# A graph network: the middle stage in pairs of tiles inside the last convolution round, and one table made in a later stage

## The reference

```python
h = jnp.maximum(_layernorm(x, axis=-1), 0.0)
x = x + _L0_gnn_ref(h, src, dst, ...)      # APPNP (5 hops), two GIN layers, mish
h = jnp.maximum(_layernorm(x, axis=-1), 0.0)
x = x + _L1_gnn_ref(h, edge_attr_3, ...)   # embedded edges, 2 x (edge MLP, sum by dst, node MLP)
h = jnp.maximum(_layernorm(x, axis=-1), 0.0)
x = x + _L2_gnn_ref(h, edge_index, ...)    # weighted sum over edges, by source
h = jnp.maximum(_layernorm(x, axis=-1), 0.0)
x = x + _L3_gnn_ref(h, src, dst, ...)      # typed features, sum by destination
```

```python
out = _gin(out, src, dst, eps2[0], W2, b2)   # ((1 + eps) * h + sum over neighbours) @ W2 + b2
return out * jnp.tanh(jax.nn.softplus(out))  # mish
```

## Time and profile before

| what | value |
|---|---|
| median of 3 runs | 4323.43 us |
| profiled execution, span | 4322.8 us |
| PE, DVE, POOL, ACT busy in the span | 73%, 59%, 49%, 31% |
| last convolution round | from 1585 us |
| middle stage | 1687.4 to 1789.2 us |
| first edge pass | 1789.2 to 2373 us |
| first node stage | 2373 to 2464 us |

### The profile page before, as it was taken

How to read it: one execution, slowest core, us unless ns; L and a number is a source line. 1 busy time by engine, 2 the same in 40 slices (tenths; PEclk the granted TensorE clock), 3 DMA queues, 4 the chain that set the end, 5 groups by cost and what they waited for, 6 DMA issues and landing times. The chain is left out here.

```text
span 4322.8 us, 75741 instructions
## 1 busy us (share of the span) xinstructions
PE 3164.4 (73%) x18619; PEld 2197.0 (51%) x18633; DVE 2559.5 (59%) x9496; ACT 1354.4 (31%) x2970; POOL 2139.2 (49%) x2173
## 2 busy tenths in 40 slices
PE   2488885669999996499998599998555555655554
PEld 1366662235666663377776367776333333333332
DVE  7688886985555554688887577776632222422223
ACT  0077886941111000255554355555300000200000
POOL 0477772000000002477774277776367777177776
PEclk7579998989999998699999799999655555755555
DMA  2112222000000002466666354455122212422223
GB/s 59 41 55 70 76 73 85 2 18 15 16 17 17 16 15 65 125 176 177 182 175 131 87 133 129 129 128 100 29 66 53 53 53 51 136 53 53 53 53 52
DMA packets 248700, 326.41 MB, mean 76 GB/s; under 512 B 78159, under 2 KB 159646, under 8 KB 247518
## 3 DMA queue, kind: packets, MB, share of 16 engines
q1 hardware_dynamic: 180122, 205.51, 15.7%
q0 software_dynamic: 68256, 117.02, 12.6%
HBM read 230.08 MB, written 92.25 MB: 75 GB/s over the span
## 5 line engine op out<-in xcount | busy, mean ns | idle before, releaser
L2506 PE MATMUL gat_acc<-gat_rows,gat_hot 128*128 128x128 f32 x1664 | 574.2, 478 | 489.1 <-issue 243.2
L2506 PEld LDWEIGHTS gat_acc<-gat_rows,gat_hot 128*128 128x128 f32 x1664 | 400.3, 317 | 664.3 <-issue 663.5
L971 PE MATMUL hop_p_a<-hop_h,adj 128*128 128x384 bf16 x4375 | 713.9, 327 | 0.0
L971 PEld LDWEIGHTS hop_p_a<-hop_h,adj 128*128 (+1 forms) x4375 | 428.7, 98 | 284.9 <-issue 2.5
L1914 POOL DMA_INDIRECT lb_far<-far_rows,lb_idx x416 | 407.2, 979 | 195.6 <-issue 118.6
L2489 POOL DMA_INDIRECT gat_rows<-typed_rows,gat_idx x416 | 396.0, 952 | 216.1 <-DVE gat_idx L2514 89.6
L2489 POOL DMA_INDIRECT gat_rows<-hidden_rows,gat_idx x416 | 395.8, 951 | 197.8 <-PE gat_acc L2506 78.0
L1914 POOL DMA_INDIRECT la_far<-far_rows,la_idx x416 | 410.5, 987 | 153.8 <-issue 117.7
L1630 POOL DMA_INDIRECT by_src_records<-scatter_rec,scatter_rank x375 | 381.6, 1018 | 129.2 <-issue 101.2
L2522 DVE TENSOR_SCALAR gat_hot<-iota_row,gat_tabs 128x128 f32<-128x128 f32 x416 | 148.6, 366 | 370.0 <-PE gat_acc L2506 363.9
L2519 DVE TENSOR_SCALAR gat_hot<-iota_row,gat_tabs 128x128 f32<-128x128 f32 x416 | 125.4, 307 | 392.7 <-PE gat_acc L2506 382.5
(11 more groups left out here) (501 smaller groups left out, 6395.6 us busy)
## 6 DMA issues: line engine op xcount, KB each, us to landing
edge_features<-emb_out SPq DMA_DIRECT2D x104, 256.0 KB
la_feat<-edge_features SPq DMA_DIRECT2D x104, 256.0 KB
edge_features<-la_out SPq DMA_DIRECT2D x104, 256.0 KB
lb_feat<-edge_features SPq DMA_DIRECT2D x104, 256.0 KB
la_place<-dst_row SPq DMA_DIRECT2D x104, 128.0 KB
lb_place<-dst_row SPq DMA_DIRECT2D x104, 128.0 KB
typed_rows<-gat_typed_row SPq DMA_DIRECT2D x25, 512.0 KB
cells_tabs<-x0share_nodes SPq DMA_DIRECT2D x125, 64.0 KB, 1.9
```

Of the source, the lines that this page charges most:

```text
L971: ins = nc.tensor.matmul(p_a[(u.par + r) % 2][:, 0:3 * D], K.adj[:, s, bass.ds(u.t * P, P)], h3[r % 2][:, s, :, :].rearrange("p i d -> p ( ...
L2506: nc.tensor.matmul(acc[:, bass.ds(at[u % LOADS], D)], hot[u % HOTS][:, :], rows[u % RING][:, :], start=False, stop=True, skip_group_check= ...
```

## The change

`gnn_input` is gone. Its work is done in `hops`, within the last round, in pairs of tiles (13 pairs, the last of one tile). The round is now written out for all 25 tiles on every engine. Buffers are cut out of the half of `h3` that the last round does not read, and so SP starts on x when the round before has been summed. Each pair's x and h are stored to DRAM (`dr.xn`, `dr.hn`) and loaded into `K.x` and `K.h` by SP in steps 1 to 21 of the first edge pass, together with the aggregate. The bias and the clip are DVE's now, and the inverse root is one power on POOL (2 columns) in place of the Newton steps. On PE the two products of a tile are one matmul of 256 columns. The tables by source are made in the first node stage: one PSUM bank is used by turns for the three transposed tables, whose transposes come in steps 3, 5 and 7 and whose copies come in steps 4, 6 and 8.

```diff
-            def gin2(u):
-                pe.wait_ge(s_a2, NT + u.t - 1)
-                products(u, HOPS + 1)
-            pipelined(pe, NT, gin2)
+            for t in range(NT + 5):
+                if t < NT:
+                    pe.wait_ge(s_a2, NT + t - 1)
+                    products(Turn(t, t % 2, t // 2, t < 2), HOPS + 1)
+                q = t // 2 - 2
+                if t % 2 == 0 and live(q):
+                    turned(q)
+                if t % 2 == 1 and live(q):
+                    weighed(q)
...
+            for t in range(2 * NP + 5):            # ACT
+                q = t // 2
+                if t % 2 == 0:
+                    norm(q - 2); high(q - 3); middle(q - 3)      # where live
+                else:
+                    exp(q); new_T(q - 2)
...
+            for q in range(NP):                    # POOL
+                c = width(q)
+                pool.wait_ge(s_num, q + 1)
+                nc.gpsimd.tensor_tensor(o[q % 2][:, 0:c, :], o[q % 2][:, 0:c, :], num[:, 0:c, :], ALU.mult).then_inc(s_on, 1)
+                pool.wait_ge(s_mish, q + 1)
+                pool.wait_ge(*x_sem(q))
+                nc.gpsimd.tensor_tensor(x_of(q), x_of(q), o[q % 2][:, 0:c, :], ALU.add).then_inc(s_x, 1)
+                pool.wait_ge(s_v, q + 1)
+                if q >= 2:
+                    pool.wait_ge(s_ln, q - 1)
+                nc.gpsimd.tensor_tensor(rstd[q % 2][:, 0:c], v[:, 0:c], K.neghalf[:, 0:c], ALU.pow).then_inc(s_root, 1)
...
+            for t in range(NT):                    # DVE
+                gin2(t)
+                q = t // 2
+                if t % 2 == 1:
+                    if live(q - 1):
+                        measured(q - 1)
+                    clipped(q)
+                    if live(q - 1):
+                        rooted(q - 1)
+                else:
+                    if live(q - 3):
+                        split_near(q - 3)
+                    if live(q - 1):
+                        mish(q - 1)
+                    if t == NT - 1:
+                        clipped(q)
+                    if live(q - 3):
+                        low(q - 3)
+            measured(NP - 2)
+            rooted(NP - 2)
+            mish(NP - 1)
+            measured(NP - 1)
+            rooted(NP - 1)
+            for q in range(NP - 3, NP):
+                split_near(q)
+                low(q)
...
+                if keeps and 1 <= g <= 3 * NB:     # SP, first edge pass
+                    t, q = (K.agg, K.h, K.x)[(g - 1) // NB], (g - 1) % NB
+                    lo, hi = QUADS[q][0], QUADS[q][-1] + 1
+                    sp.dma_start(t[:, lo:hi, :].rearrange("p t d -> p (t d)"),
+                                 (dr.agg, dr.hn, dr.xn)[(g - 1) // NB][:, lo * D:hi * D]).then_inc(s_node if g > NB else s_agg, 16)
...
+                    if keeps and g == 8:           # DVE, first edge pass
+                        dve.wait_ge(s_agg, NB * 16)
...
-                if last and r == 2:                # DVE, node stage
+                if r == 2:
                     table.vector(dve)
                 if last and r == 4:
                     table.outs(dve)
+                if not last and r in (4, 6, 8):
+                    table.outs(dve, (r - 4) // 2)
```

More of the change, by code:

```diff
@@ L506, with edge_tables @@
     pass
-def edge_tables(nc, K, dr, lay, ph, out=None, banks=None):
+def edge_tables(nc, K, dr, lay, ph, out=None, banks=None, shared=False):
     G, n_tab, S = lay.groups, lay.n_tab, lay.unit
@@ L529, in edge_tables @@
     if banks is None:
-        banks = [ph.ps(f"{lay.name}_tab_p_t{i}", [P, 4, P]) for i in range(n_tab * NB)]
+        banks = [ph.ps(f"{lay.name}_tab_p_t{i}", [P, 4, P]) for i in range(1 if shared else n_tab * NB)] * (n_tab if shared else 1)
     s_rec, s_ch, s_tab, s_tr, s_out, s_st, s_att = (ph.sem(f"{lay.name}_tab_{x}") for x in (
@@ L582, in vector, with outs @@
             nc.vector.tensor_copy(tab[:, 2, :], f(2)).then_inc(s_tab, 1)
-    def outs(dve):
-        for i in range(n_tab):
+    def outs(dve, only=None):
+        for i in range(n_tab) if only is None else (only,):
             dve.wait_ge(s_tr, i + 1)
@@ L591, in outs, with tensor @@
             ins.then_inc(s_out, 1)
-    def tensor(pe):
+    def tensor(pe, only=None):
         pe.wait_ge(s_tab, 1)
-        for i in range(n_tab):
+        for i in range(n_tab) if only is None else (only,):
+            if shared and i >= 1:
+                pe.wait_ge(s_out, i)
             for k in range(PT):
@@ L928, in hops @@
     s_a2, s_ch2 = (ph.sem(v) for v in ("gin_sum", "gin_chain"))
-    s_o = [ph.sem(f"o_stored{i}") for i in range(2)]
-    s_oc = ph.sem("o")
     dg = ph.ps("deg", [P, 32])
@@ L954, in _ @@
                 pipelined(sp, NT, load)
[L957 to L962, removed]
+                if r == 1:
+                    for j in range(2):
+                        sp.dma_start(w[:, j * D:(j + 1) * D], A["L1_gnn_eW1"][0, j * D:(j + 1) * D, :]).then_inc(s_w, 16)
+                    broadcast_row(sp, b2, A["L0_gnn_b2"], s_w)
@@ new lines, in measured @@
+            def measured(q):
+                c = width(q)
+                dve.wait_ge(s_x, q + 1)
+                for k in range(c):
+                    nc.vector.bn_stats(stats[:, k, :], x_of(q)[:, k, :]).then_inc(s_stats, 1)
+                dve.wait_ge(s_stats, PAIRS[q][-1] + 1)
+                if q >= 1:
+                    dve.wait_ge(s_rstd, q)
+                for k in range(c):
+                    nc.vector.bn_aggr(mv[:, k, :], stats[:, k, :]).then_inc(s_mv, 1)
+                dve.wait_ge(s_mv, PAIRS[q][-1] + 1)
+                nc.vector.tensor_scalar(v[:, 0:c], col(1, c), LN_EPS, None, ALU.add).then_inc(s_v, 1)
@@ L2016, in _ @@
             nc.vector.memset(K.sum[:, :, :], 0.0)
+            if keeps:
+                nc.vector.memset(K.x[:, NT:NW, :], 0.0)
             dve.wait_ge(s_w, W_LOADS * 16)
@@ L2143, in node_update @@
     PARTS = 1 if last else 2
-    table = edge_tables(nc, K, dr, dr.units, ph) if last else None
+    table = edge_tables(nc, K, dr, dr.units if last else dr.by_src, ph, shared=not last)
     LOADS = 9
@@ L2184, in _ @@
             cp = Chain(pool, s_pc)
-            if last:
-                table.gpsimd(pool)
+            table.gpsimd(pool)
             pool.wait_ge(s_ge, 16)
@@ L2279, in _ @@
                     product(r - TURN)
+                if not last and r in (3, 5, 7):
+                    table.tensor(pe, (r - 3) // 2)
         @block.scalar
```

423 lines of the change are left out of this document (191 added, 232 removed).

## The result

The changed kernel takes 4324.73 us, the median of nine runs (4322.38 to 4334.42), and the kernel before, in nine runs beside it, 4316.39 us (4312.15 to 4324.01). The ratio is 1.002, 95% interval 1.0011 to 1.003: slower by 8.3 us, where 58.8 us less were forecast. The profiled execution has the same span to a tenth as the one of before, because that one, 4323.4 us, lay 7 above the median of its nine.

What follows compares the result with a forecast made beforehand. TensorE was taken to bound the last round, at 9.0 us a pair against VectorE's 8.5. Edge pass 69.4 us earlier, less 1 for loads and 9.6 for tables, gave 58.8 less: 4323.4 to 4265, range 4255 to 4290.

Steps and rivals of the forecast that it cites:

- The wait inside it: Last round: TensorE, at a pair's transposes, waits for its normalisation; 0.6 us a pair, bounds 0 and 1.5.
- Rival (b): Last round: TensorE's waits drop the clock to 1.2 GHz, 99 us for the round, 4364 in all; chance 0.03.
- One tile, 3.95: Last round: one tile's 25 products take TensorE 3.95 us written out, so 24 steps take 94.8 instead of 97.4.
- VectorE's lists: Last round: VectorE's work per pair, 5.2 us in the even step and 3.3 in the odd, against TensorE's 9.0.
- The wait for the normalisation: Last round: TensorE waits at the transposes until ScalarE has normalised the pair; 0.6 us a pair in all.
- The power: Last round: GpSimd's inverse root on two columns takes 0.5 us, if its price goes by columns.
- rival (a): Last round and tail: GpSimd's power costs a fixed 4.3 us, 35 us more, 4300 in all; chance 0.09.
- The tail: From the last round's last sum to the first edge pass: an uncovered chain of 21.9 us, bounds 17 and 30.
- The loads in the edge pass: First edge pass: 21 more loads of 256 KB cost 1 us, bounds 0 and 12.
- rival (d): First edge pass: the added loads make gathers late, 12 us more, 4277 in all; chance 0.08.
- The first node stage: Making the tables there adds 9.6 us, bounds 5 and 11: vector part 5.2, copies 2.4, store 2.0.
- what was listed to show it right: Signs: pairs 9.6 us apart, last sum near 1698, edge pass at 1720, clock 1.00, node stage 10 longer, gather waits unchanged.

Runs made afterwards that it cites:

- e2: Changed kernel plus 25 products nobody reads on TensorE ahead of each wait for the eviction inside the round: 5200.6 us, 0.9972 of the kernel before.
- e1: Changed kernel with ScalarE's odd step evicting the transposed pair ahead of the exponential: 5158.39 us, 0.9887 of the kernel before.
- e4: Changed kernel, ScalarE's order kept, with TensorE doing a pair's weights one tile later: 5155.75 us, 0.9884 of the kernel before.
- g3: Changed kernel with eviction ahead of exponential, pair 10 split earlier in the tail, table work reordered in the first node stage: 5139.05 us, 0.9858 of the kernel before.
- h1: As g3, with GpSimd's four table gathers in halves, two behind quad 0 and two behind quad 2: 5172.17 us, 0.987 of the kernel before.
- g1: The changed kernel itself, unaltered, run again on another chip: 5222.28 us, 1.0017 of the kernel before.

## Why the prediction was wrong

**The step that failed** is in "The wait inside it". It says that behind the sum of tile 2p+3 TensorE "does the weights of the pair before (0.87)", at once. But these weights need the eviction that the same paragraph, two sentences on, puts behind the exponential ("ACT then does the exponential and an eviction"), ready at 4.1 + 0.4 + 0.4 = 4.9 by its own numbers. I used ACT's order for the normalisation, which TensorE needs a tile later, and not for the weights. Taken together the paragraph's own numbers give 4.9 + 0.87 + 3.95 + 0.22 + 3.95 = 13.9 a pair; measured at full clock (e2) it was 13.6, and in the changed kernel, with the clock, 15.9. The prediction has no term for a wait at the weights (its 0.6 a pair, bounds 0 and 1.5, is for the transposes), and that wait was 4.1 a pair. Nearly all of the miss follows: 63.9 us of the last sum (175.6 for 111.7), where the whole miss is 67.1, and e1 and e4, which cut the wait in two different ways, both come back to 109.

**Rival (b), the clock,** I gave 0.03, on the ground that TensorE would be 94% busy. That rested on the step above. The clock did fall to 0.83 in the round, and e2 shows it to be a result of the wait: filled with idle products, it stays at 1.00. It cost 23.4 us, and not the 99 that (b) had for a whole round at the lower level. The Trainium skill, "TensorE: Matmul & The Clock Gate", Part 1, says that activity releases the throttle and idleness brings it back; the windows agree (0.83 with TensorE 74% busy, 1.00 with e2's 99.6%). I had that rule right and applied it to a TensorE without the wait.

**What else was mis-sized.** None of it decides.

- *One tile, 3.95.* It is 4.06 in the written-out round, and the 2.6 us that I took off for the loop aren't there. The loop's steps alternate between 3.96 and 4.16, and I took the low one for TensorE's own. In the changed kernel one row of the timeline holds 93 products without a gap, in 15.28 us, which is 4.1 for 25. The forecast for e1's period, 2 x 4.06 + 1.09 = 9.21, then holds exactly: 1.09 was right, and so was the end of the round but for the wait.
- *VectorE's lists,* 5.2 and 3.3: measured 4.76 with its gap to the next sum, and 3.2. In e1 it keeps up.
- *The wait for the normalisation,* 0.6: nothing in e1 but 0.3 in the first pair.
- *The power,* 0.5: 0.81 on two columns, 0.56 on one, in the row of 1656.37. It doesn't go by columns alone (4.33 on 25), nor is it fixed; rival (a) is out.
- *The tail,* 21.9: 23.3. The order that I listed, pair 10 split last, was right, and g3 shows that 3.8 of it was that order's price.
- *The loads in the edge pass,* 1: nothing (582.1 after 583.7); rival (d) is out.
- *The first node stage,* 9.6, bounds 5 and 11: 12.1. The vector part costs 5.1 (5.2 forecast), the copies and small shifts 2.1 (2.4), the store at the end 2.5 (2.0). The 2.4 that are missing are the weights: I called GpSimd's gathers "hidden under the wait for weights", but they make that wait longer. The weights are there 8.8 us after the stage's first transfer instead of 6.4.
- *The base.* I summed against a profiled execution of 4323.4; nine runs have 4316.4 in the middle. As a difference, 58.8 forecast, the mended kernel has 58 to 59. That it comes so close is in part luck, since terms off by more cancel: the round of e1 is 2.8 us shorter than forecast and the loads cost 1 less, while the tail is 1.4 longer and the first node stage 2.5.

Of what was listed to show it right, only the untouched gathers of the edge pass came (in its first 116 us TensorE waited 1.7 us for gathers, before 0.6). The signs listed for a wrong one (slow power rows, VectorE without idle time, a tail beyond 30) looked at other suspects, and none of them came either: the list had no sign for a wait of TensorE for ScalarE's eviction.

## What to carry to other kernels

Where a stage is laid inside another by hand, write for every engine its list in one step, and for every instruction of the full engine both its operands' last writers and what stands before these in their own lists; an early-ready eviction queued behind a late exponential is late. Price the ring that this closes (here 13.9 us) before pricing the engines' totals (9.0 and 8.5), and add what the clock takes behind a wait of TensorE that recurs (here 2.4 us a pair on top of 4.4). When a large rearrangement brings nothing, look for the one wait of the engine that should be full: swapping two calls was worth 67 us here, more than the 58 that the whole change brings with it.

## What the runs showed of the hardware

**VectorE's small operations beside GpSimd's additions.** In the first node stage the four casts to `node_b2r` on 3 by 128 elements take 2.77 us in the changed kernel, where GpSimd adds beside them, and 0.70 in g3, where it issues gathers (the row of 2890.92). Of the changed kernel:

```profile
2383.87 2.77 DVE L1524 CAST node_b2r<-node_b2p 3x128 bf16<-3x128 f32 x4
2383.88 1.33 POOL L2209 TENSOR_TENSOR nodes_sum<-nodes_h,node_beta_row 128x512 f32<-128x512 f32 x1 [0.18 <-POOL nodes_agg L2204]
```

The bias parts together take 10.9 and 4.1. The Trainium skill, "SBUF — State Buffer", "SBUF: two separate sides", has a rule that fits: the shared port pair is locked for a whole GpSimd instruction. The trace agrees: held operations last about as long as GpSimd's (1.2 to 1.3 beside 1.26) and end with them. Beside the rows of gathers the same operations are short, with one exception: in h1 an operation that begins beside a gather's row (2916.28) ends only with the addition behind it, 1.97 later.

**Scattering and the other queue.** On the chips of the later runs the embedding stage all but stops for most of the time in which GpSimd issues its 375 scatters (176 to 674 us). Of the changed kernel, the first chip first, then g1's:

```profile
400.00:640.00 240.00, 205.21 (x1305) 161.10 (x1306) 201.23 (x962) 202.26 (x421) 184.23 (x184) 0.91 0.23 73
```

```profile
200.00:640.00 440.00, 54.45 (x189) 38.03 (x187) 26.68 (x137) 25.28 (x49) 331.94 (x332) 0.50 0.03 4
```

GpSimd issues at the same rate on both (a scatter's row is 0.97), but all DMA of the core together moves 4 GB/s instead of 73 in these stretches, and the stage's stores run from 433 to 1126 us instead of 228 to 661. The first edge pass takes 726 instead of 582 there. It is the same program; what differs between the chips the runs don't show, and whether the scatters are the cause wasn't tried.
